# Attention's products on pairs of 16-bit floats, and the causal mask added by VectorE with the row maximum

## The chip, the cores and the metric

One NeuronCore of one Trainium2 chip runs the whole program in a single launch. The metric is the device time of that launch in microseconds (us), less is better. TensorE (PE) multiplies, with its weight loads (PEld) shown apart; VectorE (DVE), ScalarE (ACT) and GpSimd (POOL) do elementwise work; SyncE (SP) issues the DMAs.

## The reference

The program is a macaron block on 8 sequences of 1024 tokens with 256 features: half a feed-forward step, attention, half a feed-forward step. The feed-forward quantises its inputs and weights to 4-bit floats in blocks of 16. Cut to what matters here:

```
def _L0_attn_ref(query, Wq, Wk, Wv, Wo, span_val):      # 16 heads of 64
    q, k, v = (_split_heads(query @ W) for W in (Wq, Wk, Wv))
    w = jnp.einsum('bhqd,bhkd->bhqk', q, k) / DH
    w = w + causal                                      # -1e9 above the diagonal
    w = softmax(w) * clip((arange(s) + span_val * s) / 33, 0, 1)
    w = w / (sum(w) + 1e-8)
    return merge_heads(einsum('bhqk,bhkd->bhqd', w, v)) @ Wo

x = x + 0.5 * ffn(layernorm(x)); x = x + attn(layernorm(x)); x = x + 0.5 * ffn(layernorm(x))
```

## The kernel before

The program has three stages: a first feed-forward pass (`ffn_pass`, tag `ffn1`), attention (`attention`), and a second feed-forward pass (`ffn2`). A feed-forward pass works through 32 macros of 256 tokens. While the first pass runs, `prepare` splits the attention weights in hooks of its steps: ScalarE rounds a chunk of 128x512 to the high half (`hi_of`, L1034), GpSimd subtracts it from the chunk to get the low half (`split`, L835), and SyncE stores both to DRAM (`store`, L762). There are 16 such chunks, one per step from step 0 on. The chunks of Wv and Wo are first scaled by a power of two (L1040) that is derived from the largest element of Wv (`largest_v`, L919, and `powers`, L923).

Attention goes through 8 sequences times 8 pairs of heads, 64 pairs in all (`over_pairs`, L1102). All products are made of a high and a low part: high by high, high by low, low by high. The operands of the projections, of the scores and of the output product are rounded 32-bit words (`F32R`); the operands of the product with the values (`v_cols`, `eT`) are already 16-bit floats (`F16`). Each pair has 16 units, one for each head and each tile j of 128 query rows; a unit's scores have 128(j+1) columns, since the mask is causal. Per unit:

- `scores` (L1343) waits until the exponential of the unit two before has read the same PSUM buffer (`exp_done`, L1350). It makes the scores in one or two chunks of 256 to 512 columns, each as two matmuls, since the keys' low and high halves are stacked on the 128 partitions (L1356, L1357). A third matmul, a 16-bit identity by a 128x128 block of 0 and -1e9, adds the mask to the diagonal block (L1360).
- `row_max` (L1538) is VectorE's reduction of the scores to the negated row maximum (L1542).
- `exp` (L1448) is ScalarE's exponential, from PSUM into `e_rows`, with that as its bias (L1455).
- `turn` (L1363) transposes the rows on TensorE in groups of up to four 128x128 blocks, 24 groups a pair, as 32-bit words (L1370). ScalarE rounds a group to `eT_hi` (`turn_hi`, L1462), VectorE subtracts to get `eT_lo` (`turn_lo`, L1548), and three groups later `value` (L1373) multiplies both by the values (L1386, 132 and 66 columns).

Between them lie ten side pieces a pair, which share one PSUM bank (`side_ps`): two each of q and k for the next pair (`project`, L1285, six matmuls of 512 columns each), two transposes of the output (L1324), and four of values (L1297) or of the output product (L1334), twelve matmuls of 256 columns each. A side piece is copied by ScalarE (high part, L1435) and finished by VectorE (low part, L1510, or L1524, L1536) before the next may use the bank. The pieces of q and k go by DMA to the stacked layout (`place`, L1124).

The order of all this work is a table of steps that each engine runs in its own queue: `pair_steps` (L618) puts the side pieces into numbered slots (`WO_SLOTS`, `V_SLOTS`, `FRESH_SLOTS`, L585 to L587), and in the first pair of a sequence 14 small steps of normalising the next rows are added to VectorE's queue (`norm_x`, L1561).

## Time and profile before

| | |
|---|---|
| time, median of 3 runs | 3530.09 us (3526.44 to 3532.24) |
| span of the profiled execution, first to last instruction | 3527.3 us; no other time of that execution is given |
| busy: TensorE, VectorE, ScalarE, GpSimd | 96%, 83%, 67%, 24% |
| mean granted clock of TensorE | 0.988 |
| DMA | 375.19 MB, mean 106 GB/s |
| chain that ended last | PE 64%, DVE 10%, issue 6%, ACT 2%, POOL 2% |

A row of TensorE gives a duration with the pipeline's latency in it, so neighbouring matmuls overlap. What a matmul costs is read from one start to the next. The same holds in a smaller measure for VectorE.

### The profile page before, as it was taken

The numbers are of one execution on the slowest core, as the hardware profiler recorded it, in microseconds if no ns is written. First come the engines' busy times: TensorE is split into PE (matmuls) and PEld (weight loads), VectorE is DVE, ScalarE is ACT, GpSimd is POOL, SyncE is SP. The second block draws the span as 40 slices with busy tenths as digits, with TensorE's granted clock in tenths as the row PEclk, the third lists the DMA queues.
The fourth block names the chain that finished last, engine by engine and source line by source line (L and its number), as shares of the span: only waits on it lengthen the run. The fifth ranks groups of instructions, "written<-read, shape, count | busy, mean of one in ns | idle before, by whom it ended". The sixth has DMA issues, their size and how long they took to land.

```text
span 3527.3 us, 77883 instructions
## 1 busy us (share of the span) xinstructions
PE 3383.0 (96%) x29872; PEld 3071.4 (87%) x29872; DVE 2916.8 (83%) x4672; ACT 2350.8 (67%) x4307; POOL 848.4 (24%) x911
## 2 busy tenths in 40 slices
PE   4999996999999999999999999999999999799998
PEld 4999995888888888888888888888888888699998
DVE  8999974888888888888888878878887888899996
...
GB/s 123 95 123 87 93 33 124 97 117 125 125 109 126 109 142 125 112 125 122 109 126 137 116 109 134 125 103 141 134 98 107 145 104 153 54 49 55 55 54 37
DMA packets 160338, 375.19 MB, mean 106 GB/s; under 512 B 19824, under 2 KB 62832, under 8 KB 159728
## 3 DMA queue, kind: packets, MB, share of 16 engines
...
## 4 chain that ended last, share of the span: by engine, by line
PE 64%; DVE 10%; issue 6%; ACT 2%; POOL 2%; POOLq 0%; ACTq 0%; DVEq 0%
PE at_t_ps L1370 11%; PE at_side_ps L1285 9%; PE at_o_ps L1386 8%; PE ffn_gu_ps L505 7%; PE at_s_ps L1356 6%; PE at_s_ps L1357 6%; PE at_side_ps L1297 5%; PE at_side_ps L1334 4%; PE ffn_down_ps L530 4%; DVE at_neg_max L1542 3%; DVE at_eT_lo L1548 3%; PE at_s_ps L1360 1%; PE ffn_hT_ps L475 1%; PE at_side_ps L1324 1%; DVE at_oT_lo L1510 1%
## 5 line engine op out<-in xcount | busy, mean ns | idle before, releaser
L1548 DVE SCALAR_TENSOR_TENSOR at_eT_lo<-at_t_ps,at_eT_hi 128x512 f16<-128x512 f32 (+3 forms) x1536 | 852.2, 555 | 328.8 <-ACT at_eT_hi L1462 322.9
L1462 ACT ACTIVATE at_eT_hi<-at_t_ps 128x512 f16<-128x512 f32 (+3 forms) x1536 | 756.7, 493 | 333.3 <-PE at_t_ps L1370 322.6
L1455 ACT ACTIVATE at_e_rows<-at_s_ps,at_neg_max 128x1024 f32<-128x1024 f32 (+7 forms) x1024 | 759.7, 742 | 152.2 <-DVE at_neg_max L1542 144.7
L1370 PE MATMUL at_t_ps<-at_ident,at_e_rows 128*128 128x128 f32 x4608 | 798.8, 284 | 0.0
L1542 DVE TENSOR_REDUCE at_neg_max<-at_s_ps 128x1 f32<-128x1024 f32 (+7 forms) x1024 | 766.1, 748 | 19.4 <-PE at_s_ps L1360 15.6
L1386 PE MATMUL at_o_ps<-at_v_cols,at_eT_hi 128*128 128x132 f16 x4608 | 611.5, 222 | 2.1 <-DVE at_eT_lo L1548 1.6
L1356 PE MATMUL at_s_ps<-at_kh_st,at_q_st 128*128 128x512 f32 (+2 forms) x1536 | 583.0, 380 | 19.0 <-issue 9.1
L1386 PE MATMUL at_o_ps<-at_v_cols,at_eT_lo 128*128 128x66 f16 x4608 | 567.2, 192 | 0.0
L1357 PE MATMUL at_s_ps<-at_kl_st,at_q_st 128*128 128x512 f32 (+2 forms) x1536 | 514.1, 342 | 0.0
L1370 PEld LDWEIGHTS at_t_ps<-at_ident,at_e_rows 128*128 128x128 f32 x4608 | 491.7, 141 | 0.1
L1386 PEld LDWEIGHTS at_o_ps<-at_v_cols,at_eT_hi 128*128 128x128 f16 x4608 | 432.5, 98 | 25.7 <-issue 18.8
L1386 PEld LDWEIGHTS at_o_ps<-at_v_cols,at_eT_lo 128*128 128x128 f16 x4608 | 420.8, 98 | 4.0
L1285 PE MATMUL at_side_ps<-at_xT_hi,at_w_qk 128*128 128x512 f32 x1012 | 382.3, 418 | 6.5 <-DVE at_xT_lo L1510 1.4
L1356 PEld LDWEIGHTS at_s_ps<-at_kh_st,at_q_st 128*128 128x128 f32 x1536 | 295.5, 192 | 46.2 <-issue 13.5
L1244 POOL TENSOR_TENSOR at_o_sum<-at_o_raw 128x1056 f32<-128x1056 f32 x64 | 133.1, 2080 | 753.8 <-ACT at_o_raw L1473 753.8
L1357 PEld LDWEIGHTS at_s_ps<-at_kl_st,at_q_st 128*128 128x128 f32 x1536 | 292.8, 191 | 24.1
L385 POOL TENSOR_TENSOR ffn_h_q<-ffn_code,ffn_scale 128x704 f32<-128x704 f32 x128 | 178.0, 1392 | 561.8 <-DVE ffn_code L313 561.8
L505 PE MATMUL ffn_gu_ps<-ffn_w_gu_hi,ffn_xT_hi 128*128 128x352 f32 x1024 | 257.6, 333 | 25.1 <-DVE ffn_raw L276 15.7
L1473 ACT ACTIVATE at_o_raw<-at_o_ps 128x264 f32<-128x264 f32 x512 | 203.0, 396 | 76.9 <-PE at_o_ps L1386 75.7
L505 PE MATMUL ffn_gu_ps<-ffn_w_gu_lo,ffn_xT_hi 128*128 128x352 f32 x1024 | 250.6, 327 | 0.0
L505 PE MATMUL ffn_gu_ps<-ffn_w_gu_hi,ffn_xT_lo 128*128 128x352 f32 x1024 | 250.3, 326 | 0.0
L442 ACT ACTIVATE ffn_silu<-ffn_gu_ps 128x704 f32<-128x704 f32 x128 | 97.2, 760 | 214.4 <-PE ffn_gu_ps L505 214.4
...
## 6 DMA issues: line engine op xcount, KB each, us to landing
at_kh_st<-at_k_hi SPq DMA_DIRECT2D x256, 256.0 KB, 4.5
at_kl_st<-at_k_lo SPq DMA_DIRECT2D x256, 256.0 KB, 5.9
...
at_q_st<-at_q_hi SPq DMA_DIRECT2D x128, 256.0 KB, 3.8
at_q_st<-at_q_lo SPq DMA_DIRECT2D x128, 256.0 KB, 4.8
...
```

The costliest lines, as they stand in the source:

```text
L385: nc.gpsimd.tensor_tensor(blocks_of(h_q[:, par, j, :INNER]), blocks_of(code[:, j * INNER:(j + 1) * INNER]), per_block(scale[:, par, j * HB ...
L505: last = nc.tensor.matmul(gu_ps[:, c, 0:HALF_I], xT[a][:, par, kt, j * P:(j + 1) * P], gu[b][:, kt, c * HALF_I:(c + 1) * HALF_I], start=n ...
L1285: last = nc.tensor.matmul(bank[:], wts[:, w, s, kt, :], xT[t][:, kt, c * CHUNK:(c + 1) * CHUNK], start=i == 0, stop=i == len(passes) - 1)
L1356: nc.tensor.matmul(out, qs, kh_st[par][a][:, k0:k0 + w], start=True, stop=False)
L1357: last = nc.tensor.matmul(out, qs, kl_st[par][a][:, k0:k0 + w], start=False, stop=not lastc)
L1370: last = nc.tensor.transpose(t_ps[i % TBUF][:, b * P:(b + 1) * P], e_rows[:, n % 4, (k0 + b) * P:(k0 + b + 1) * P], ident[:])
L1386: last = nc.tensor.matmul(o[:, :VPART[s]], eT[s][:, i % EBUF, b * P:(b + 1) * P], v_cols[par][:, k0 + b, a, :VPART[s]], start=k0 + b == 0 ...
L1455: nc.scalar.activation(e_rows[:, n % 4, :w], s_ps[n % 2][:, col:col + w], ACT.Exp, bias=neg_max[:, n % 4:n % 4 + 1]).then_inc(sem("exp_don ...
L1462: nc.scalar.activation(eT[0][:, i % EBUF, :count * P], t_ps[i % TBUF][:, :count * P], ACT.Copy, scale=PSCALE).then_inc(sem("eT_hi"), 1)
L1473: nc.scalar.activation(o_raw[:, a * QT + j0:a * QT + j1 + 1:j1 - j0, :], o_ps[n // OSET % OBUF][:, :2 * VCOLS].rearrange("p (u d) -> p u d ...
L1542: nc.vector.tensor_reduce(neg_max[:, n % 4:n % 4 + 1], s_ps[n % 2][:, col:col + P * (j + 1)], AX.X, ALU.max, negate=True).then_inc(sem("ma ...
L1548: nc.vector.scalar_tensor_tensor(out=eT[1][:, i % EBUF, :count * P], in0=t_ps[i % TBUF][:, :count * P], scalar=PSCALE, in1=eT[0][:, i % EB ...
```

## The change

- The weights of q, k, v and o, the turned rows, q, k and their stacked copies, and the turned output become pairs of `F16` in place of pairs of `F32R`. All four weight matrices are scaled by powers of two (`flip`), the turned rows by 2^10; the scales are taken back in `s_scale` (scores), the mask of the values, and `o_scale` (output product, which becomes a scalar_tensor_tensor on VectorE).
- The largest element is now taken of all four matrices (four reductions on VectorE, two each in steps 1 and 2), and the splitting of the weights starts 6 steps later (`PA_FIRST`), with one scaling on ScalarE for each of the 16 chunks, not for 8. The steps written out before the loop grow from 20 to 24.
- The chunks of the scores are 512 columns and the rest, down to 128; the mask matmul is gone. q is negated, and VectorE makes scores times scale plus a strip (0, and a large positive number above the diagonal) into `e_rows` in one tensor_tensor_reduce that also gives the minimum. ScalarE's exponential then reads and writes `e_rows`. `scores` waits for `max_done` of the unit two before, no longer for `exp_done`; the wait for the free row of `e_rows` moves from ScalarE to VectorE.

```
-HEAD = 5 * UNROLL
+HEAD = 6 * UNROLL
...
 def score_chunks(j):
     w = P * (j + 1)
-    if w <= CHUNK:
-        return [(0, 0, max(w, 2 * P))]
-    first = CHUNK if w - CHUNK >= 2 * P else w - 2 * P
-    return [(CHUNK - first, 0, first), (CHUNK, first, w - first)]
+    return [(0, 0, w)] if w <= CHUNK else [(0, 0, CHUNK), (CHUNK, CHUNK, w - CHUNK)]
...
-    half = [[sb(f"{part}{s}", [P, CHUNK], F32R) for s in range(PA_SLOTS)] for part in ("hi", "lo")]
+    half = [[sb(f"{part}{s}", [P, CHUNK], F16) for s in range(PA_SLOTS)] for part in ("hi", "lo")]
...
         def third_out():
-            largest_v()
+            largest_of(0)
+            largest_of(1)
             scaled(4)
+        def other_largest():
+            largest_of(2)
+            largest_of(3)
...
-            if i >= 2:
-                act.wait_ge(sem("powers"), 1)
-                nc.scalar.activation(chunk(c), chunk(c), ACT.Copy, scale=(flip if i == 2 else unscale)[:, 0:1]).then_inc(sem("even"), 1)
+            act.wait_ge(sem("powers"), 1)
+            nc.scalar.activation(chunk(c), chunk(c), ACT.Copy, scale=flip[:, i:i + 1]).then_inc(sem("even"), 1)
...
-                **{(c, "normed"): (lambda c=c: hi_of(c)) for c in range(2, len(PA_CHUNKS))}}
+                **{(c + PA_FIRST, "normed"): (lambda c=c: hi_of(c)) for c in range(len(PA_CHUNKS))}}
...
-        xT = [sb(f"xT_{part}", [P, KT, SEQ], F32R) for part in ("hi", "lo")]
-        side = {n: [sb(f"{n}_{part}", [P, SEQ], F32R) for part in ("hi", "lo")] for n in "qk"}
-        q_st, kh_st, kl_st = ([[sb(f"{n}{i}{a}", [P, SEQ], F32R) for a in range(2)] for i in range(2)] for n in ("q_st", "kh_st", "kl_st"))
+        xT = [sb(f"xT_{part}", [P, KT, SEQ], F16) for part in ("hi", "lo")]
+        side = {n: [sb(f"{n}_{part}", [P, SEQ], F16) for part in ("hi", "lo")] for n in "qk"}
+        q_st, kh_st, kl_st = ([[sb(f"{n}{i}{a}", [P, SEQ], F16) for a in range(2)] for i in range(2)] for n in ("q_st", "kh_st", "kl_st"))
+        strip = sb("strip", [P, SEQ])
...
-                pe.wait_ge(sem("exp_done"), g * NU + (n - 1 + AHEAD["exp_done"]))
+                pe.wait_ge(sem("max_done"), g * NU + (n - 1 + AHEAD["max_done"]))
...
-                    last = nc.tensor.matmul(out, qs, kl_st[par][a][:, k0:k0 + w], start=False, stop=not lastc)
-                    if lastc:
-                        diag = col + j * P - k0
-                        last = nc.tensor.matmul(s_ps[n % 2][:, diag:diag + P], ident_b[:], causal[:], start=False, stop=True)
+                    last = nc.tensor.matmul(out, qs, kl_st[par][a][:, k0:k0 + w], start=False, stop=True)
...
-                act.wait_ge(sem("turned"), g * NG + (LAST_GROUP[(n - 4) % NU] + 1 + (n - 4) // NU * NG + AHEAD["turned"]))
-                nc.scalar.activation(e_rows[:, n % 4, :w], s_ps[n % 2][:, col:col + w], ACT.Exp, bias=neg_max[:, n % 4:n % 4 + 1]).then_inc(sem("exp_done"), 1)
+                nc.scalar.activation(e_rows[:, n % 4, :w], e_rows[:, n % 4, :w], ACT.Exp, bias=neg_max[:, n % 4:n % 4 + 1],
+                                     scale=-1.0).then_inc(sem("exp_done"), 1)
...
-                nc.vector.tensor_reduce(neg_max[:, n % 4:n % 4 + 1], s_ps[n % 2][:, col:col + P * (j + 1)], AX.X, ALU.max,
-                                        negate=True).then_inc(sem("max_done"), 1)
+                dve.wait_ge(sem("turned"), g * NG + (LAST_GROUP[(n - 4) % NU] + 1 + (n - 4) // NU * NG + AHEAD["turned"]))
+                nc.vector.tensor_tensor_reduce(e_rows[:, n % 4, :w], s_ps[n % 2][:, col:col + w], strip[:, SEQ - w:], keep["s_scale"][:, 0:1], BIGGEST,
+                                               ALU.add, ALU.min, neg_max[:, n % 4:n % 4 + 1]).then_inc(sem("max_done"), 1)
```

How the instructions stand on the engines. First TensorE, at the scores of a unit with 640 columns (j = 4), and the first of the value products behind them (`at_kh_st` and `at_kl_st` are the stacked keys; numbers behind names are the builder's). Before:

```order
L1356 MATMUL at_s_ps<-at_kh_st_6933,at_q_st_6929 128x384
L1357 MATMUL at_s_ps<-at_kl_st_6937,at_q_st_6929 128x384
L1356 MATMUL at_s_ps<-at_kh_st_6933,at_q_st_6929 128x256
L1357 MATMUL at_s_ps<-at_kl_st_6937,at_q_st_6929 128x256
L1360 MATMUL at_s_ps<-at_causal,at_ident_b 128x128
L1386 MATMUL at_o_ps<-at_v_cols_6943,at_eT_hi 128x132
```

and now:

```order
L1366 MATMUL at_s_ps<-at_kh_st_7431,at_q_st_7427 128x512
L1367 MATMUL at_s_ps<-at_kl_st_7435,at_q_st_7427 128x512
L1366 MATMUL at_s_ps<-at_kh_st_7431,at_q_st_7427 128x128
L1367 MATMUL at_s_ps<-at_kl_st_7435,at_q_st_7427 128x128
L1393 MATMUL at_o_ps<-at_v_cols_7442,at_eT_hi 128x132
L1393 MATMUL at_o_ps<-at_v_cols_7442,at_eT_lo 128x66
```

The same 640 columns are taken in chunks of 512 and 128, and the third matmul is gone.

Second VectorE, in the middle of a pair that has q, k and value pieces (`at_den` and `at_rden` are the row sums and their reciprocals). Before:

```order
L1548 SCALAR_TENSOR_TENSOR at_eT_lo<-at_t_ps,at_eT_hi 128x512
L1559 RECIPROCAL at_rden<-at_den 128x16
L1548 SCALAR_TENSOR_TENSOR at_eT_lo<-at_t_ps,at_eT_hi 128x384
L1510 SCALAR_TENSOR_TENSOR at_k_lo<-at_side_ps,at_k_hi 128x512
L1542 TENSOR_REDUCE at_neg_max<-at_s_ps 128x1
L1548 SCALAR_TENSOR_TENSOR at_eT_lo<-at_t_ps,at_eT_hi 128x512
L1542 TENSOR_REDUCE at_neg_max<-at_s_ps 128x1
L1548 SCALAR_TENSOR_TENSOR at_eT_lo<-at_t_ps,at_eT_hi 128x512
```

and now:

```order
L1556 SCALAR_TENSOR_TENSOR at_eT_lo<-at_t_ps,at_eT_hi 128x512
L1567 RECIPROCAL at_rden<-at_den 128x16
L1556 SCALAR_TENSOR_TENSOR at_eT_lo<-at_t_ps,at_eT_hi 128x384
L1514 SCALAR_TENSOR_TENSOR at_k_lo<-at_side_ps,at_k_hi 128x512
L1550 ISA at_e_rows,at_neg_max<-at_s_ps,at_strip,keep_s_scale 128x384
L1550 ISA at_neg_max 128x1
L1556 SCALAR_TENSOR_TENSOR at_eT_lo<-at_t_ps,at_eT_hi 128x512
L1550 ISA at_e_rows,at_neg_max<-at_s_ps,at_strip,keep_s_scale 128x1024
L1550 ISA at_neg_max 128x1
L1556 SCALAR_TENSOR_TENSOR at_eT_lo<-at_t_ps,at_eT_hi 128x512
```

Each reduction has become two instructions in VectorE's queue, of which the second writes the minimum alone; their places between the `eT_lo` rows are the same.

Third VectorE in the first feed-forward pass, at the end of its step 1 (`prep_raw_wv` is Wv as loaded). Before:

```order
L296 RECIPROCAL ffn_recip<-ffn_tied 128x120
L299 TENSOR_TENSOR ffn_unit<-ffn_raw,ffn_recip 128x1920
L921 TENSOR_REDUCE prep_big<-prep_raw_wv 128x1
L255 BN_STATS ffn_stats<-ffn_x_rows 128x6 x2
L259 BN_AGGR ffn_moments<-ffn_stats 128x2 x2
L261 TENSOR_SCALAR ffn_var_eps<-ffn_moments 128x2
```

and now:

```order
L296 RECIPROCAL ffn_recip<-ffn_tied 128x120
L299 TENSOR_TENSOR ffn_unit<-ffn_raw,ffn_recip 128x1920
L921 TENSOR_REDUCE prep_big<-prep_raw_wq 128x1
L921 TENSOR_REDUCE prep_big<-prep_raw_wk 128x1
L255 BN_STATS ffn_stats<-ffn_x_rows 128x6 x2
L259 BN_AGGR ffn_moments<-ffn_stats 128x2 x2
```

Two reductions stand where there was one, and two more follow at the end of the next step.

## Rows read from the trace of the kernel before

**Rows 1.** The page: span, and busy time by engine.
```profile
span 3527.3 us, 77883 instructions
...
PE 3383.0 (96%) x29872; PEld 3071.4 (87%) x29872; DVE 2916.8 (83%) x4672; ACT 2350.8 (67%) x4307; POOL 848.4 (24%) x911
```

**Rows 2.** Windows by stage: start:end, length, busy us (x instructions) of PE, PEld, DVE, ACT, POOL; clock, DMA share, GB/s.
```profile
60.00:500.00 440.00, 430.14 (x3061) 425.02 (x3062) 415.83 (x477) 268.29 (x374) 158.41 (x161) 0.99 0.28 89
...
580.00:3010.00 2430.00, 2401.11 (x22978) 2109.72 (x22976) 1971.78 (x3509) 1753.88 (x3470) 504.35 (x536) 1.00 0.49 122
...
3040.00:3527.00 487.00, 464.49 (x3331) 457.71 (x3329) 431.63 (x497) 269.16 (x371) 142.26 (x150) 0.99 0.16 49
```

**Rows 3.** Windows of the length of one sequence (8 pairs), amid attention; columns as above.
```profile
1000.00:1304.00 304.00, 301.14 (x2887) 264.70 (x2886) 247.69 (x443) 219.68 (x435) 64.72 (x69) 1.00 0.49 122
```

**Rows 4.** Timeline of TensorE amid attention: start us, us, engine, line, what, count.
```profile
1500.93 0.22 PE L1386 MATMUL at_o_ps<-at_v_cols,at_eT_hi 128*128 128x132 f16 x1
...
1501.28 0.63 PE L1370 MATMUL at_t_ps<-at_ident,at_e_rows 128*128 128x128 f32 x4
1501.66 0.48 PE L1285 MATMUL at_side_ps<-at_xT_hi,at_w_qk 128*128 128x512 f32 x1
1501.98 0.39 PE L1285 MATMUL at_side_ps<-at_xT_lo,at_w_qk 128*128 128x512 f32 x1
...
1502.68 0.39 PE L1285 MATMUL at_side_ps<-at_xT_lo,at_w_qk 128*128 128x512 f32 x1
...
1503.83 0.28 PE L1357 MATMUL at_s_ps<-at_kl_st,at_q_st 128*128 128x256 f32 x1
1503.95 0.23 PE L1360 MATMUL at_s_ps<-at_causal,at_ident_b 128*128 128x128 bf16 x1
1504.02 0.22 PE L1386 MATMUL at_o_ps<-at_v_cols,at_eT_hi 128*128 128x132 f16 x1
...
1504.28 0.30 PE L1370 MATMUL at_t_ps<-at_ident,at_e_rows 128*128 128x128 f32 x1
1504.72 0.50 PE L1285 MATMUL at_side_ps<-at_xT_hi,at_w_qk 128*128 128x512 f32 x1
```

**Rows 5.** Groups by line over the span: ... xcount, busy us, mean ns of one, idle before.
```profile
L1356 PE MATMUL at_s_ps<-at_kh_st,at_q_st 128*128 128x512 f32 (+2 forms) x1536 | 583.0, 380 | 19.0 <-issue 9.1 <-ACT at_e_rows L1455 6.4 <-DVE at_acc L1536 3.5
...
L1360 PE MATMUL at_s_ps<-at_causal,at_ident_b 128*128 128x128 bf16 x1024 | 235.8, 230 | 0.0
...
L1356 PEld LDWEIGHTS at_s_ps<-at_kh_st,at_q_st 128*128 128x128 f32 x1536 | 295.5, 192 | 46.2 <-issue 13.5 <-DVE at_acc L1536 4.9 <-ACT at_e_rows L1455 4.3
...
L1386 PEld LDWEIGHTS at_o_ps<-at_v_cols,at_eT_hi 128*128 128x128 f16 x4608 | 432.5, 98 | 25.7 <-issue 18.8 <-DVE at_eT_lo L1548 2.9
```

**Rows 6.** Timeline of VectorE amid attention.
```profile
1503.97 0.69 DVE L1510 SCALAR_TENSOR_TENSOR at_q_lo<-at_side_ps,at_q_hi 128x512 fp32r<-128x512 f32 x1 [0.70 <-ACT at_q_hi L1435]
...
1516.08 0.68 DVE L1548 SCALAR_TENSOR_TENSOR at_eT_lo<-at_t_ps,at_eT_hi 128x512 f16<-128x512 f32 x1
1516.68 1.21 DVE L1542 TENSOR_REDUCE at_neg_max<-at_s_ps 128x1 f32<-128x1024 f32 x1
1517.89 0.69 DVE L1548 SCALAR_TENSOR_TENSOR at_eT_lo<-at_t_ps,at_eT_hi 128x512 f16<-128x512 f32 x1
...
1531.95 0.63 DVE L1571 BATCH_NORM_AGGREGATE at_moments<-at_stats 128x2 f32<-128x6 f32 x8
```

**Rows 7.** Groups by line over the span: VectorE, a PSUM and an SBUF operand.
```profile
L1536 DVE TENSOR_TENSOR at_acc<-at_side_ps,at_acc 128x512 f32<-128x512 f32 x125 | 85.7, 686 | 6.3 <-PE at_side_ps L1334 0.7
```

**Rows 8.** Timeline of VectorE in step 1 of the first feed-forward pass.
```profile
67.56 2.28 DVE L921 TENSOR_REDUCE prep_big<-prep_raw_wv 128x1 f32<-128x2048 f32 x1
69.76 0.74 DVE L255 BATCH_NORM_STATS2 ffn_stats<-ffn_x_rows 128x6 f32<-128x256 f32 x2
```

**Rows 9.** Timelines at attention's start: SyncE's issues and TensorE's first scores.
```profile
569.80 2.93 SPq L1130 DMA_DIRECT2D at_kl_st<-at_k_lo  x4
...
579.53 0.77 PE L1356 MATMUL at_s_ps<-at_kh_st,at_q_st 128*128 128x512 f32 x1 [9.10 <-issue]
```

More of the change, by code:

```diff
@@ L225, in body @@
                     load_rows(i + UNROLL, k)
-                if isinstance(i, int) and UNROLL <= i < HEAD and not reload:
+                if isinstance(i, int) and UNROLL <= i < UNROLL + 16 and not reload:
                     keep_weights(i - UNROLL)
@@ L571 @@
 SUM_EPS = 1e-8
+BIGGEST = 3.0e38
+XSCALE = 2.0 ** 10
+EARLY, LATE = 60 * 1024, 132 * 1024
 PSCALE = 2.0 ** 14
@@ L768, in store @@
             for part in range(2):
-                cols = half[part][c % PA_SLOTS][:].bitcast(F32)
+                cols = half[part][c % PA_SLOTS][:]
                 if i < 2:
@@ L793, in before_step @@
                 spread_largest()
-            if step >= 2:
-                store(step - 2)
+            if step >= PA_FIRST + 2:
+                store(step - PA_FIRST - 2)
         def all_stored():
@@ L818, in sync @@
         return {START: first_loads, "rows": other_loads, MACROS - UNROLL + 1: first_sequence, "end": first_loaded,
-                **{step: (lambda step=step: before_step(step)) for step in range(1, len(PA_CHUNKS) + 2)}}
+                **{step: (lambda step=step: before_step(step)) for step in range(1, PA_FIRST + len(PA_CHUNKS) + 2)}}
     def gpsimd(pool):
@@ L960, in first_norm @@
                                         ALU.subtract, ALU.mult).then_inc(sem("xn_first"), 1)
-        return {START: first_two, LAST: first_norm, -3: lambda: to_codes(1), -2: lambda: scaled(2), (0, "rows out"): third, 1: third_out, 6: powers}
+        return {START: first_two, LAST: first_norm, -3: lambda: to_codes(1), -2: lambda: scaled(2), (0, "rows out"): third, 1: third_out, 2: other_largest, 6: powers}
     def tensor(pe):
@@ L1129, in place @@
                         for a in range(2):
-                            sp.dma_start(st[par][a][half * DH:(half + 1) * DH, :].bitcast(F32),
-                                         side[n][part][a * DH:(a + 1) * DH, :].bitcast(F32)).then_inc(sem(f"{n}_placed{par}"), 16)
+                            sp.dma_start(st[par][a][half * DH:(half + 1) * DH, :],
+                                         side[n][part][a * DH:(a + 1) * DH, :]).then_inc(sem(f"{n}_placed{par}"), 16)
             def start():
@@ L1394, in start @@
                         pe.wait_ge(sem("xT_lo"), 4)
-                    out.append(piece(kind, c, 0, 0, 0, 1, out[n - 4] if n >= 4 else ("consts", 3), start_ps[n % 4]))
+                    out.append(piece(kind, c, 0, 0, 0, 1, out[n - 4] if n >= 4 else ("consts", 1), start_ps[n % 4]))
                 scores(0, 0, 0)
@@ L1439, in piece @@
                 if kind in ("q", "k"):
-                    copy_side(side[kind][0][:, cols], f"{kind}_done", 2 * g + (c + 1), f"{kind}_hi", 1.0 / DH if kind == "q" else 1.0, bank)
+                    copy_side(side[kind][0][:, cols], f"{kind}_done", 2 * g + (c + 1), f"{kind}_hi", (-1.0 if kind == "q" else 1.0) / XSCALE, bank)
                 elif kind == "o_turn":
@@ L1509, in split_side @@
                 dve.wait_ge(sem(ready), count)
-                nc.vector.scalar_tensor_tensor(out=out, in0=bank[:], scalar=scale, in1=hi.bitcast(F32),
+                nc.vector.scalar_tensor_tensor(out=out, in0=bank[:], scalar=scale, in1=hi,
                                                op0=ALU.mult, op1=ALU.subtract).then_inc(sem(signal), 1)
@@ L1516, in piece @@
                     hi, lo = side[kind]
-                    split_side(lo[:, cols], hi[:, cols], f"{kind}_hi", 2 * g + (c + 1), f"{kind}_lo", 1.0 / DH if kind == "q" else 1.0, bank)
+                    split_side(lo[:, cols], hi[:, cols], f"{kind}_hi", 2 * g + (c + 1), f"{kind}_lo", (-1.0 if kind == "q" else 1.0) / XSCALE, bank)
                 elif kind == "v":
@@ L1531, in piece @@
                     out = [xT[s][:, c // 2, (c % 2) * CHUNK:(c % 2 + 1) * CHUNK] for s in range(2)]
-                    split_side(out[1], out[0], "xT_hi", g + (c + 1), "xT_lo", 1.0, bank)
+                    split_side(out[1], out[0], "xT_hi", g + (c + 1), "xT_lo", XSCALE, bank)
                 elif kind == "wo":
@@ L1535, in piece @@
                     rows = acc[:, 2 * c:2 * c + 2, :].rearrange("p j k -> p (j k)")
-                    nc.vector.tensor_tensor(rows, bank[:], rows, ALU.add).then_inc(sem("wo_added"), 1)
+                    nc.vector.scalar_tensor_tensor(out=rows, in0=bank[:], scalar=keep["o_scale"][:, 0:1], in1=rows,
+                                                   op0=ALU.mult, op1=ALU.add).then_inc(sem("wo_added"), 1)
             def row_max(n, g):
@@ L1617, in _ @@
             nc.vector.memset(power[:], -0.5).then_inc(sem("power"), 1)
-            for name in ("eT_lo", "wo_added"):
+            dve.wait_ge(sem("masked"), 2)
+            for name in ("eT_lo", "wo_added", "max_done"):
                 dve.sem_inc(sem(name), AHEAD[name])
```

104 lines of the change are left out of this document (56 added, 48 removed).

## The prediction

> **What bounds the kernel now.** I read the page first for the whole: in a span of 3527.3 us TensorE is busy for 96% and VectorE for 83% [rows 1]. A mean over three stages says little, so the windows by stage come next [rows 2]. The reader is to see that attention takes some 2430 of 3527 us, that TensorE is busy for 2401 us of them at a granted clock of 1.00 (the 2.4 GHz level), and that VectorE is busy for 1972. Both feed-forward passes have TensorE busy for nearly all of their steady part, with VectorE close behind: 415.8 of 440 us. One sequence, 8 pairs, takes exactly 304 us, window after window, so a pair takes 38.0 us; in it VectorE is busy for 247.7/8 = 31.0 us and ScalarE for 27.5 [rows 3]. The timeline of TensorE shows why it is the bound [rows 4]: matmuls start one behind the other, and gaps in which it waits for others are short. So a pair is worth what its matmuls cost from start to start, as long as nobody else becomes slower than TensorE.
>
> **TensorE, per pair.** From starts to starts [rows 4]: three matmuls of rounded words with 512 columns take 0.70 us from 1501.98 to 1502.68, 0.233 each. One with 256 columns takes 0.12. Four pairs of 16-bit matmuls with 132 and 66 columns take 0.35 us from 1500.93 to 1501.28, 0.0875 a pair. At 2.4 GHz, a column a cycle, 198 columns are 0.0825, so each 16-bit matmul has about 3 ns on top. I take N/2.4 + 3 ns for 16 bits: 0.216 us for 512 columns, 0.163 for 384, 0.110 for 256, 0.056 for 128. No row has 16-bit matmuls of 512 columns in this kernel, so the bounds are 0.213 (a column a cycle) and 0.233 (as the rounded words).
> - The projections of q and k have 4 pieces of 6 matmuls: 24 x (0.233 - 0.216) = 0.41 us.
> - Values or output product, 4 pieces of 12 matmuls: 48 x (0.120 - 0.110) = 0.48 us.
> - Scores: per head 12 chunks, each twice (L1356 counts 1536, 24 a pair [rows 5]). Before, a pair has 20 matmuls of 512 columns, 12 of 384 (0.177, midway between the two rows) and 16 of 256: 4.66 + 2.12 + 1.92 = 8.70 us. Now 24 of 512, 8 each of 384, 256 and 128: 5.18 + 1.30 + 0.88 + 0.45 = 7.81 us. Saved: 0.89 us.
> - Mask: 16 matmuls a pair (1024 in all [rows 5]), 0.07 us from 1503.95 to 1504.02 [rows 4]: 1.1 us.
> - First matmul after transposes: the one at 1501.66 takes 0.32 us to the next start, not 0.233 [rows 4], since its weight load takes 192 ns where a 16-bit one takes 98 [rows 5], and a transpose ahead of it (0.11 each) hides only the shorter. The value matmuls after transposes show no such step. In the timeline about 18 of a pair's 24 groups of such matmuls begin behind transposes: 18 x 0.087 = 1.55 us.
>
> Sum: 4.4 us a pair, 282 us over 64 pairs. With 16-bit matmuls as slow per column as rounded words only the mask, the weight loads and the 512 columns fewer (0.22 us) are left, 2.9 us.
>
> The Trainium skill ("TensorE: Matmul & The Clock Gate", section "Back-to-back issue gap") gives N/2.4 + 2.5 ns for a lone kind of matmul, but about 81 ns at 128 columns for real streams of weight loads and matmuls. By the latter the eight 128-column matmuls would cost 0.2 us a pair more, 13 us in all; the trace has 0.0875 for two 16-bit matmuls with their loads, and sides with the former.
>
> **VectorE, per pair.** The reduction turns into two instructions (the order shows `at_e_rows,at_neg_max` and then `at_neg_max` alone). For the main one the nearest row is one that takes PSUM and SBUF in and writes SBUF: 686 ns at 512 columns [rows 7], as `eT_lo` and `q_lo` take [rows 6]; the reduction itself takes 1.21 us for 1024 columns, so all run at one element a cycle with the same constant. I book no difference. The second, tiny one is nowhere in this trace. Eight aggregations of 6 elements take 0.63 us, 0.08 each [rows 6], the lower bound. If it has to wait until the main one has drained, the next instruction loses the overlap too (1516.08 to 1516.68 is 0.60 for an instruction of 0.68, so 0.08), and a small instruction takes 0.17: 0.25, the upper bound. I take 0.12, nearer the row. 16 x 0.12 = 1.9 us, with bounds of 1.3 and 4.0: VectorE is then busy for 32.9 us a pair. The output product's addition keeps its length, a multiplication more in the same pass.
>
> **What is late next.** TensorE alone would need 38.0 - 4.4 = 33.6 us, VectorE 32.9. They are now level, and two waits grow. First the side pieces: they share one bank, and the next may start only when VectorE is done with the last. Here TensorE starts one transpose at 1504.28 and the next q piece only at 1504.72 [rows 4], 0.33 us beyond the 0.11 of the transpose, because `q_lo` ran from 1503.97 to 1504.66 [rows 6]. With less other work between, such places wait longer by what that work shrank: some 3 places a pair by 0.1 us, 0.3 us. Second VectorE's queue, at 94% load: `eT_lo` and `max_done` come later where 1024-column units and side pieces meet. I take 0.9 us (0 if the three groups between turn and value absorb it, 2.6 if VectorE with some idle time sets the pace). A pair takes 38.0 - 4.4 + 1.2 = 34.8 us: 3.2 us less, 205 us in 64 pairs. In the first pair of seven of the sequences VectorE has normalisation on top, about 5 us by its rows of 0.41 us and less; it is the bound there: 1.5 us each, 10 us.
>
> **Edits off that path.** ScalarE reads SBUF and not PSUM in the exponential, and has 10 us of slack a pair: nothing, hidden under TensorE. The scores no longer wait for the exponential; that wait hardly shows (6.4 us over the span [rows 5]), so nothing. DMAs halve, off the path except at the start: `place` is issued until 572.73, the scores begin at 579.53 [rows 9]; half the bytes save 4 us (0 to 7). The strip's set-up on GpSimd adds under 1 us, inside that. In the first pass VectorE gets three more reductions of 2.2 us (67.56 to 69.76 [rows 8]) at steps 1 and 2, where it is the bound, and some 1.5 us in `powers`: 7 us (3 to 9), since VectorE's slack in a step is small. Eight more scalings on ScalarE, busy 268 of 440 us [rows 2], and later stores on SyncE's and splits on GpSimd's queues cost nothing: all is stored by step 23, and attention loads it at step 29.
>
> **Sum.** 3527.3 - 205 + 10 - 4 + 7 = 3335 us for the profiled execution. Its span lies 2.8 us under the median of the runs, 3530.1, so the median is put at 3338 us.
>
> **The rivals.**
> - Everything absorbed: queues and bank cost nothing, 3527 - 282 + 3 = 3248, 3251 as a median. For it speaks that TensorE waits little today with VectorE at 82%; against, the wait at 1504.28 that is there already.
> - VectorE the bound: the small instruction costs 0.25 us, VectorE needs 35.0 us a pair and with some idle time the pair takes 36.2: 1.8 x 64 = 115 less, 3527 - 115 + 13 = 3425, median 3428. It decides from about 0.16 us on, where VectorE's sum passes TensorE's.
> - 16 bits no faster per column: 2.9 - 1.2 = 1.7 us a pair, 109 us, 3431, median 3434.
> - Slower than before: the new main instruction takes two cycles an element. Mean length is 576 columns, 0.6 us more in each of 16, 9.6 us a pair: VectorE 31.0 + 1.9 + 9.6 = 42.5 us busy, less 1.5 of overlap, so pairs of 41 us: 3527 + 192 + 13 = 3732, median 3735. It turns slower from some 0.45 us an instruction on. For it: nothing here scales, adds and reduces in one pass. Against it: each of its parts runs at full rate, and PSUM and SBUF together do too [rows 7]. The Trainium skill ("Vector Engine (DVE) Microarchitecture Reference", section "Points that are easy to get wrong") says that such a form with two 32-bit SBUF sources runs at half throughput; here one source is PSUM, so by its wording the rule would not bite, and no run here shows it.
>
> **How the numbers follow.** Forecast 0.50, all absorbed 0.14, VectorE the bound 0.17, 16 bits no faster 0.10, half rate 0.07; 0.02 for anything else. The likeliest is 3338 us. Its own range, 3290 to 3385, is reached out to the rivals on the faster side: 3255 to 3445 leaves out the half rate and a little at each end. A measurement tells 0.2% (7 us) from no change. Faster by more than that: 0.92; within: 0.01; slower: 0.07.
>
> **What would show it.** In the profile after: 16-bit matmuls of 512 columns starting 0.216 us apart, first ones after transposes without the 0.09 step, no mask rows; the new main rows near 1.22 us at 1024 columns and the small rows behind them at 0.08 to 0.17; a sequence of 278 to 282 us; VectorE busy for over 90% of it; TensorE's waits for `eT_lo`, `q_lo` and `k_lo` grown to about 1 us a pair. The prediction is wrong if main rows are near 2.3 us, if a sequence takes over 290 us, or if the first pass grows by more than 10 us.

## The result, and the profile after

The changed kernel takes 3453.35 us (median of 4 runs, 3450.93 to 3454.41) against 3529.8 us before: a ratio of 0.9782, with a 95% interval of 0.9768 to 0.9796. It is 76 us faster. The forecast was 3338 us, 192 us faster, with a range up to 3445 us: the sign was right, the size was not, and the result lies above the range.

The page of the kernel after, span and engines (to [rows 1]):

```profile
span 3452.6 us, 76458 instructions
...
PE 3223.7 (93%) x28848; PEld 2677.1 (78%) x28848; DVE 2967.2 (86%) x5704; ACT 2367.8 (69%) x4315; POOL 845.1 (24%) x910
```

Windows of the kernel after, columns as in [rows 2, 3]; the last is one sequence of 8 pairs:

```profile
60.00:500.00 440.00, 427.75 (x3019) 422.51 (x3020) 416.63 (x478) 272.19 (x381) 153.81 (x160) 0.98 0.24 74
...
1000.00:1296.00 296.00, 282.93 (x2769) 217.36 (x2768) 254.43 (x574) 221.68 (x437) 64.50 (x69) 0.99 0.28 69
```

All of the gain lies in attention. The first low part `eT_lo` starts at 587.5 us before and 586.8 after, the last one at 3013.3 and 2937.4: 75 us less between them. Ahead of it two changes cancel. The last instruction of the first feed-forward pass on VectorE, before and then after:

```profile
536.53 0.69 DVE L322 SCALAR_TENSOR_TENSOR ffn_x_out<-ffn_down_ps,ffn_x_res 128x512 f32<-128x512 f32 x1 [8.81 <-PE ffn_down_ps L530]
```

```profile
543.11 0.69 DVE L322 SCALAR_TENSOR_TENSOR ffn_x_out<-ffn_down_ps,ffn_x_res 128x512 f32<-128x512 f32 x1 [8.77 <-PE ffn_down_ps L530]
```

The pass ends 6.6 us later, and from there to the first scores it takes 38.0 us (543.11 to 581.13) and not 43.0 (536.53 to 579.53 [rows 9]). The starts of `eT_lo`, 24 to a pair, give the length of each pair. A plain pair took 37.4 to 37.7 us and takes 36.0 to 36.2. The first pair of a sequence took 39.2 and takes **39.7** (39.5 to 40.2). The seventh, with the transposes of the next sequence's x, went from 40.8 to 39.2. A whole sequence went from 305.1 to some 296 us. TensorE's busy sum is 282.9 of the 296 us; before it was 301.1 of 304 [rows 3]. VectorE is busy for 254.4 of them, 86%. So TensorE has waits that it did not have: over the span the waits that the trace names ahead of its matmuls in attention add up to 53 us before and 142 after, 1.4 us more a pair. Those that VectorE ended went from 11 to 102 us.

Waits over the span, first of the kernel before (us in total, times, longest), then of the kernel after:

```profile
PEld at_side_ps L1324 <- DVE at_oT_lo L1510: 24.4, 63, 0.4
...
PE at_side_ps L1324 <- DVE at_oT_lo L1510: 1.8, 7, 0.3
```

```profile
ACT at_e_rows L1458 <- DVE at_neg_max L1550: 319.3, 558, 10.2
DVE at_eT_lo L1556 <- ACT at_eT_hi L1466: 246.7, 524, 0.9
...
PE at_side_ps L1334 <- DVE at_oT_lo L1514: 47.9, 63, 1.0
...
PE at_s_ps L1366 <- DVE at_acc L1540: 12.5, 6, 2.1
...
PE at_side_ps L1344 <- DVE at_acc L1540: 11.0, 31, 0.7
...
PE at_side_ps L1295 <- DVE at_q_lo L1514: 9.7, 35, 0.6
PE at_side_ps L1307 <- DVE at_v_masked L1528: 9.2, 31, 0.3
```

The second output transpose (L1334) now waits in every pair for VectorE to let go of the side bank. The timelines around one such place, after, VectorE and then TensorE:

```profile
1633.39 0.69 DVE L1514 SCALAR_TENSOR_TENSOR at_k_lo<-at_side_ps,at_k_hi 128x512 f16<-128x512 f32 x1
1634.00 0.61 DVE L1550 CUSTOM_DVE_ANT_0 at_e_rows<-at_s_ps,at_strip,keep_s_scale 128x384 f32<-128x384 f32 x1
1634.53 0.09 DVE L1550 DVE_READ_ACCUMULATOR2_ANT at_neg_max<- 128x1 f32 x1
1634.53 0.69 DVE L1556 SCALAR_TENSOR_TENSOR at_eT_lo<-at_t_ps,at_eT_hi 128x512 f16<-128x512 f32 x1
1635.13 1.27 DVE L1550 CUSTOM_DVE_ANT_0 at_e_rows<-at_s_ps,at_strip,keep_s_scale 128x1024 f32<-128x1024 f32 x1
1636.33 0.08 DVE L1550 DVE_READ_ACCUMULATOR2_ANT at_neg_max<- 128x1 f32 x1
1636.33 0.69 DVE L1556 SCALAR_TENSOR_TENSOR at_eT_lo<-at_t_ps,at_eT_hi 128x512 f16<-128x512 f32 x1
1636.94 0.68 DVE L1514 SCALAR_TENSOR_TENSOR at_oT_lo<-at_side_ps,at_oT_hi 128x512 f16<-128x512 f32 x1
1637.79 0.29 DVE L1556 SCALAR_TENSOR_TENSOR at_eT_lo<-at_t_ps,at_eT_hi 128x128 f16<-128x128 f32 x1 [0.18 <-ACT at_eT_hi L1466]
```

```profile
1634.84 0.60 PE L1334 MATMUL at_side_ps<-at_ident,at_o_norm 128*128 128x128 f32 x4
...
1636.14 0.52 PE L1377 MATMUL at_t_ps<-at_ident,at_e_rows 128*128 128x128 f32 x3
...
1637.67 0.66 PE L1334 MATMUL at_side_ps<-at_ident,at_o_norm 128*128 128x128 f32 x4 [1.00 <-DVE at_oT_lo L1514]
```

ScalarE had `oT_hi` ready at 1636.24 (0.59 us from 1635.65), but VectorE has no gap from 1633.39 to 1637.62, and `oT_lo` gets its turn at 1636.94. Elsewhere in the same pair VectorE stands idle, some 5 us in all.

The new instruction by form, after (count, busy us, mean ns), and the output product's addition:

```profile
L1550 DVE CUSTOM_DVE_ANT_0 at_e_rows<-at_s_ps,at_strip,keep_s_scale 128x1024 f32<-128x1024 f32 x128 | 163.3, 1276 | 5.6 <-PE at_s_ps L1367 4.8
...
L1540 DVE SCALAR_TENSOR_TENSOR at_acc<-at_side_ps,keep_o_scale,at_acc 128x512 f32<-128x512 f32 x125 | 92.9, 744 | 0.6 <-PE at_side_ps L1344 0.6
L1550 DVE DVE_READ_ACCUMULATOR2_ANT at_neg_max<- 128x1 f32 x1024 | 85.0, 83 | 0.0
```

### The profile page after: what moved, and what is told of

It reads as the page before. It is cut to its first block, busy times and chain, and to the rows that moved or that the text cites. A ratio compares the mean times of both kernels' runs of the same rounds, so it can differ in the third digit from the quotient of the medians.

```text
span 3452.6 us, 76458 instructions
## 1 busy us (share of the span) xinstructions
PE 3223.7 (93%) x28848; PEld 2677.1 (78%) x28848; DVE 2967.2 (86%) x5704; ACT 2367.8 (69%) x4315; POOL 845.1 (24%) x910
## 4 chain that ended last, share of the span: by engine, by line
PE 42%; DVE 17%; issue 16%; ACT 7%; POOL 2%; DVEq 0%; ACTq 0%; POOLq 0%
DVE at_e_rows L1550 8%; PE ffn_gu_ps L505 7%; PE at_side_ps L1295 7%; PE at_t_ps L1377 6%; PE at_o_ps L1393 5%; DVE at_eT_lo L1556 4%; ACT at_eT_hi L1466 4%; PE ffn_down_ps L530 4%; PE at_s_ps L1366 3%; PE at_s_ps L1367 3%; PE at_side_ps L1344 3%; PE at_side_ps L1307 1%; DVE at_v_masked L1528 1%; PE ffn_hT_ps L475 1%; DVE at_oT_lo L1514 1%
## 5 line engine op out<-in xcount | busy, mean ns | idle before, releaser
L1458 ACT ACTIVATE at_e_rows<-at_e_rows,at_neg_max 128x1024 f32<-128x1024 f32 (+7 forms) x1024 | 791.5, 773 | 321.3 <-DVE at_neg_max L1550 319.3
L1466 ACT ACTIVATE at_eT_hi<-at_t_ps 128x512 f16<-128x512 f32 (+3 forms) x1536 | 742.8, 484 | 158.3 <-PE at_t_ps L1377 144.7
L1550 DVE CUSTOM_DVE_ANT_0 at_e_rows<-at_s_ps,at_strip,keep_s_scale 128x1024 f32<-128x1024 f32 (+7 forms) x1024 | 827.7, 808 | 7.0 <-PE at_s_ps L1367 6.2
L1366 PE MATMUL at_s_ps<-at_kh_st,at_q_st 128*128 128x512 f16 (+3 forms) x1536 | 502.2, 327 | 18.3 <-DVE at_acc L1540 12.5
L1367 PE MATMUL at_s_ps<-at_kl_st,at_q_st 128*128 128x512 f16 (+3 forms) x1536 | 481.9, 327 | 0.0
L1295 PE MATMUL at_side_ps<-at_xT_hi,at_w_qk 128*128 128x512 f16 x1012 | 344.5, 381 | 12.7 <-DVE at_q_lo L1514 9.7
L1366 PEld LDWEIGHTS at_s_ps<-at_kh_st,at_q_st 128*128 128x128 f16 x1536 | 154.7, 101 | 106.5 <-DVE at_acc L1540 13.9
L1259 POOL TENSOR_TENSOR at_o_norm<-at_o_sum,at_rden 128x1024 f32<-128x1024 f32 x64 | 122.0, 1906 | 435.6 <-DVE at_rden L1567 435.6
L1247 POOL CAST at_v_cols<-at_v_masked 128x512 f16<-128x512 f32 x128 | 78.3, 612 | 597.9 <-DVE at_v_masked L1528 597.9
```

What stands on the lines that cost most here:

```text
L1295: last = nc.tensor.matmul(bank[:], wts[:, w, s, kt, :], xT[t][:, kt, c * CHUNK:(c + 1) * CHUNK], start=i == 0, stop=i == len(passes) - 1)
L1366: nc.tensor.matmul(out, qs, kh_st[par][a][:, k0:k0 + w], start=True, stop=False)
L1367: last = nc.tensor.matmul(out, qs, kl_st[par][a][:, k0:k0 + w], start=False, stop=True)
L1458: nc.scalar.activation(e_rows[:, n % 4, :w], e_rows[:, n % 4, :w], ACT.Exp, bias=neg_max[:, n % 4:n % 4 + 1], scale=-1.0).then_inc(sem("ex ...
L1466: nc.scalar.activation(eT[0][:, i % EBUF, :count * P], t_ps[i % TBUF][:, :count * P], ACT.Copy, scale=PSCALE).then_inc(sem("eT_hi"), 1)
L1550: nc.vector.tensor_tensor_reduce(e_rows[:, n % 4, :w], s_ps[n % 2][:, col:col + w], strip[:, SEQ - w:], keep["s_scale"][:, 0:1], BIGGEST, ...
```

## The experiments

Four readings stood against each other. **A**: the step of 0.087 us behind transposes [rows 4] was never there to save, and about 1.4 us a pair come back as waits. **B**: the steps were saved, and all that is missing are waits. **C**: TensorE is the bound throughout, and VectorE's time does not matter. **D**: VectorE's sum of work decides.

### One half of the change at a time

`only_16bit` keeps TensorE's mask, the plain maximum and the exponential out of PSUM, with q and k scaled by constants that hold for this input:

```diff
-                nc.vector.tensor_tensor_reduce(e_rows[:, n % 4, :w], s_ps[n % 2][:, col:col + w], strip[:, SEQ - w:], ...
+                nc.vector.tensor_reduce(neg_max[:, n % 4:n % 4 + 1], s_ps[n % 2][:, col:col + w], AX.X, ALU.max, negate=True)...
+                    if lastc:
+                        last = nc.tensor.matmul(s_ps[n % 2][:, diag:diag + P], ident_b[:], causal[:], start=False, stop=True)
```

> The 16-bit pairs alone: mask by TensorE and plain row maximum as in the kernel before. Theory A (no step behind transposes was ever there to save, TensorE's own saving is 1.8 us a pair here, some 0.4 us of it comes back as waits at the side bank): 1.4 us x 64 = 90 us less than before, about 3440 us. Rival B (the step of 0.087 us was real and was saved, all that is missing in the changed kernel are waits that VectorE makes): TensorE saves 3.3 us a pair, 0.7 comes back, 165 us less, about 3365 us. In the trace A has the last transpose and the first matmul behind it together at 0.325 us before the next start (0.348 before the change).

Measured: 3433.7 us (3433.0 to 3434.4), ratio 0.9724 [0.9708, 0.9741], 97 us less than before and **20 us less than the whole change**. Reading A named 3440, B 3365. Its trace settles the step; TensorE, four transposes and what follows:

```profile
1640.35 0.63 PE L1380 MATMUL at_t_ps<-at_ident,at_e_rows 128*128 128x128 f32 x4
1640.82 0.38 PE L1366 MATMUL at_s_ps<-at_kh_st,at_q_st 128*128 128x512 f16 x1
1641.03 0.38 PE L1367 MATMUL at_s_ps<-at_kl_st,at_q_st 128*128 128x512 f16 x1
```

From the first transpose to the second 512-column matmul it is 0.68 us here, and was 0.70 before (1501.28 to 1501.98 [rows 4]). The difference is what the 512 columns save (0.233 to 0.216), and nothing more. In [rows 4] the first matmul indeed takes 0.32 us to the next start, but it starts 0.08 us early, 0.38 behind the first of the four transposes. In nearly every place of the trace of the kernel before, a rounded matmul stands 0.39 behind the first of four transposes, and a 16-bit value matmul 0.47. With 16 bits the matmul of the scores starts 0.47 behind too, and takes 0.21. The record had moved the 0.087 us from one row to the next.

`only_mask` is the other half: rounded words kept, the mask and the maximum in one VectorE instruction, with a column of ones as scale.

```diff
-                    if lastc:
-                        diag = col + j * P - k0
-                        last = nc.tensor.matmul(s_ps[n % 2][:, diag:diag + P], ident_b[:], causal[:], start=False, stop=True)
+                nc.vector.tensor_tensor_reduce(e_rows[:, n % 4, :w], s_ps[n % 2][:, col:col + w], strip[:, SEQ - w:], one[:, 0:1], BIGGEST, ...
```

> The mask and the maximum in one VectorE instruction alone, products on rounded 32-bit words kept. TensorE has 16 mask matmuls a pair less (1.0 us), VectorE 1.9 us a pair more. Theory A (waits at the side bank and in the first pair of a sequence take what VectorE adds): 0 to 0.4 us a pair less, 3505 to 3530 us. Rival C (VectorE's time never matters while it is below TensorE's): 1.0 us a pair less, 3466 us. Rival D (VectorE's queue decides fully): 0.9 us a pair more, 3588 us.

Measured: 3511.0 us (3509.3 to 3511.7), ratio 0.9942 [0.9925, 0.9958], 19.5 us less, 0.3 us a pair. TensorE's 1.0 us a pair is mostly given back; on rounded words both C and D fall. The halves alone give 97 and 19.5 us, together 76: on top of the 16-bit pairs the fused mask, with its scale read from a column, **costs** 20 us.

### What a microsecond is worth on each engine

`immediate` gives the two scales as constants of the instruction instead of columns in SBUF; they hold for this input:

```diff
-  nc.vector.scalar_tensor_tensor(out=rows, in0=bank[:], scalar=keep["o_scale"][:, 0:1], in1=rows,
+  nc.vector.scalar_tensor_tensor(out=rows, in0=bank[:], scalar=2.0 ** -16, in1=rows,
...
-  nc.vector.tensor_tensor_reduce(..., strip[:, SEQ - w:], keep["s_scale"][:, 0:1], BIGGEST,
+  nc.vector.tensor_tensor_reduce(..., strip[:, SEQ - w:], 2.0 ** -22, BIGGEST,
```

> The changed kernel with the two scales as constants of the instruction instead of a column in SBUF. Theory A: each of 16 maxima and of the output additions loses its 60 ns, VectorE has 1.1 us a pair less, of which a third to a half is on the path: 20 to 35 us under the changed kernel, 3420 to 3433. Rival D (VectorE decides fully): 1.1 us x 64 = 70 us, 3383. If the 60 ns are not from the column but from the custom instruction itself, only the additions shorten and the time stays within 5 us of 3453.

Measured: 3413.0 us (3410.9 to 3413.8), ratio 0.9666 [0.965, 0.9682], 40 us under the changed kernel, a little more than A's 20 to 35. The trace of `immediate`, VectorE by form:

```profile
L1550 DVE CUSTOM_DVE_ANT_0 at_e_rows<-at_s_ps,at_strip 128x1024 f32<-128x1024 f32 x128 | 155.6, 1216 | 5.9 <-PE at_s_ps L1367 5.9
...
L1540 DVE SCALAR_TENSOR_TENSOR at_acc<-at_side_ps,at_acc 128x512 f32<-128x512 f32 x125 | 85.7, 686 | 0.9 <-PE at_side_ps L1344 0.6
L1550 DVE DVE_READ_ACCUMULATOR2_ANT at_neg_max<- 128x1 f32 x1024 | 85.4, 83 | 0.1
```

1216 ns for 1276, 686 for 744: reading the scale from a column costs 60 ns an instruction, whatever its length. That is 1.1 us a pair on VectorE, and 0.63 us of it were on the path. With constants the fused mask gains 21 us over `only_16bit`, instead of costing 20. A little of the 21 is not the mask's: `only_16bit` still reads `o_scale` from a column, two additions of 60 ns a pair.

`zero_mask` puts 16 mask matmuls a pair back, which add zeros:

```diff
+                    if lastc:
+                        diag = col + j * P - k0
+                        last = nc.tensor.matmul(s_ps[n % 2][:, diag:diag + P], ident_b[:], zeros[:], start=False, stop=True)
```

> The changed kernel with 16 mask matmuls a pair put back that add zeros: 1.0 us a pair more for TensorE, nothing for VectorE. Theory A (TensorE waits about 2 us a pair at the side bank, work between two side pieces fills part of it): 0.4 to 0.7 us a pair more, 3480 to 3498. Rival C (TensorE is the bound throughout): 1.0 us a pair, 3517. Rival D (VectorE decides): under 0.2 us a pair, under 3465.

Measured: 3462.7 us (3459.7 to 3467.8), ratio 0.9811 [0.9795, 0.9827]: 9 us more, 0.15 us a pair for 0.9 us of TensorE's work (16 starts, 0.056 us each in this trace). C wanted 64 us. For the changed kernel D now looked best, and A had TensorE too dear.

### Where the waits are made

The next two move side pieces. The numbers are places among a pair's 24 groups:

```diff
-WO_SLOTS = (0, 2, 4, 7, 9, 11, 14, 15, 19, 21)
-V_SLOTS = (2, 3, 5, 7, 9, 11, 14, 16, 20, 21)
+WO_SLOTS = (0, 2, 4, 7, 9, 12, 15, 17, 19, 21)
+V_SLOTS = (2, 3, 5, 7, 9, 12, 15, 17, 19, 21)
```

That is `slots_o`. `slots_q` has the same last six places and 0, 3, 5, 7 ahead of them in both tables.

> The changed kernel with the second output transpose one step later (place 12 instead of 11, so 2.6 us of TensorE's work instead of 1.2 lie between the two), and the four pieces behind it at 15, 17, 19, 21. Theory A (the returned time is waits of TensorE at the one side bank, 1.0 us a pair at this place): 0.6 to 0.9 us a pair less, 3395 to 3415 us. Rival D (VectorE's sum decides, as a scale of 60 ns an instruction was worth 40 us and 1.0 us of TensorE's only 9): the wait moves elsewhere, within 12 us of 3453.

> As the one before, and the projections of q and k at places 0, 3, 5, 7 in every pair (2.7 us of TensorE's work between the first two, not 1.1 or 1.5). Theory A: another 0.1 to 0.4 us a pair less, 3375 to 3405 us. Rival D: within 12 us of 3453.

Measured: `slots_o` 3441.6 us (3441.0 to 3442.9), ratio 0.9747 [0.9731, 0.9764]; `slots_q` 3445.6 us (3445.3 to 3446.7), ratio 0.9759 [0.9743, 0.9775]. Only 12 and 8 us less, against 40 to 75 expected, and within the 12 that D named. The wait of the second output transpose had gone, and two others stood in its place. A row of TensorE's timeline in `slots_o`, and its waits over the span:

```profile
1630.27 0.22 PE L1393 MATMUL at_o_ps<-at_v_cols,at_eT_hi 128*128 128x132 f16 x1 [0.87 <-DVE at_eT_lo L1556]
```

```profile
PE at_o_ps L1393 <- DVE at_eT_lo L1556: 41.6, 60, 1.7
PE at_o_ps L1393 <- ACT at_o_raw L1477: 33.8, 64, 1.0
```

The value product now waits for `eT_lo`, which stands in the same full queue of VectorE, and for ScalarE's copy out of the one bank of output sums. A was wrong on where the time is made: freeing the side bank at this place does not give it back.

`slots_even` spaces all ten pieces, at 0, 3, 6, 9, 12, 15, 18, 20, 21, 23:

> The changed kernel with the ten side pieces at 0, 3, 6, 9, 12, 15, 18, 20, 21, 23: at least 2.6 us of TensorE's work behind each that goes through ScalarE and VectorE, but the last addition close to the next pair's first piece. Theory A: 3375 to 3420 us. Rival D: within 12 us of 3453.

Measured: 3552.7 us (3552.1 to 3554.0), ratio 1.006 [1.0044, 1.0077], **slower than before the change**, so neither reading holds. TensorE's waits there:

```profile
PE at_o_ps L1393 <- ACT at_o_raw L1477: 106.8, 231, 1.0
...
PE at_o_ps L1393 <- DVE at_eT_lo L1556: 24.5, 60, 1.7
```

The copy `o_raw` follows the last value product of a pair of units, at places 2, 5, 8, 11, 14, 17, 20 and 23, and the next product into that bank comes one place later. A side piece at such a place gives TensorE something to do meanwhile. The old tables have three and five pieces there, those of `slots_o` two and three, `slots_even` two. The count alone does not decide: `slots_q` has two as well, and waits 57.6 us for `o_raw`, in 119 places. Of the 99 us that `slots_even` takes over the changed kernel, the waits for `o_raw` are 100 (6.4 us there), and 25 more stand ahead of scores with no releaser named; waits for VectorE are 29 us fewer.

That gave a fifth reading, **E**: VectorE has 31 of 36 us of work, but it is full in some stretches and idle in others. The time is made in the full ones. I laid the three queues side by side with the durations of the trace, the copies among them, and chose 1, 3, 5, 8, 9, 11, 13, 15, 18, 21 for all pairs.

> The changed kernel with the ten side pieces at 1, 3, 5, 8, 9, 11, 13, 15, 18, 21 in every pair. Theory E, formed after the last runs (in a plain pair VectorE has 31 of 36 us, but its queue is without a gap in the stretch that holds the 1024-column maximum, the last low part of k and both output transposes, and elsewhere it idles; the returned time is made in such stretches, and where TensorE waits, at the bank or for the low part, is only where it shows): pieces that give TensorE much and VectorE little, put where VectorE is full, and none two steps apart around place 10 to 12, give 0.8 to 1.3 us a pair, 3370 to 3405 us. Rival D (VectorE's sum counts, wherever it is): within 12 us of slots_o, 3430 to 3453.

> The same with the 16 mask matmuls a pair that add zeros, 1.0 us more for TensorE. Theory E: with VectorE's full stretches relieved TensorE is the bound over more of the pair, so 0.4 to 0.9 us a pair more than slots_odd (25 to 58 us), where the changed kernel had 0.15. Rival D: as there, under 12 us more.

Measured: `slots_odd` 3411.5 us (3404.6 to 3412.8), ratio 0.9665 [0.9649, 0.9681], 42 us under the changed kernel with the same instructions on every engine; D allowed 12 to either side of `slots_o`, and it lies 30 under. Plain pairs take 35.15 us. It came 7 us above E's range, since the first pair of a sequence did not shrink with the others and takes 40.0 us. `slots_odd_zero` 3440.1 us (3436.1 to 3441.4), ratio 0.9743 [0.9726, 0.9759]: TensorE's 0.9 us now costs 29 us, 0.45 a pair, three times as much as in the old order. No run changes VectorE's queue and the cover of the copies one at a time, but the waits over the span, added up by who ended them, tell them apart. From the changed kernel to `slots_odd`, TensorE's waits for VectorE fall from 102 to 64 us, and those for `o_raw` rise from 6.4 to 8.7. That is 36 of the 42 us, all of it waits for VectorE. The copies took from `slots_o` what the new places had won there (VectorE 78 us, `o_raw` 33.8); they are not what the changed kernel lacked.

### The first pair of a sequence

After the change, TensorE at the end of a first pair, and the windows there (columns as above):

```profile
1506.63 0.52 PE L1377 MATMUL at_t_ps<-at_ident,at_e_rows 128*128 128x128 f32 x3
1509.23 0.39 PE L1366 MATMUL at_s_ps<-at_kh_st,at_q_st 128*128 128x512 f16 x1 [2.08 <-DVE at_acc L1540]
...
1510.24 1.09 PE L1377 MATMUL at_t_ps<-at_ident,at_e_rows 128*128 128x128 f32 x4
```

```profile
1492.00:1502.00 10.00, 9.37 (x100) 7.76 (x98) 9.78 (x26) 6.95 (x13) 0.00 (x0) 1.00 0.08 24
1502.00:1512.00 10.00, 7.92 (x80) 6.66 (x79) 9.85 (x32) 5.56 (x12) 1.81 (x2) 0.91 0.18 42
```

VectorE is busy for 9.8 of 10 us. TensorE waits 2.08 us at the next pair's head for the last addition, and here the granted clock then falls: four transposes take 1.09 us, not 0.63. It does not always fall. The trace has six such places, each with a wait of 2.08 us. Behind four of them transposes start some 0.21 us apart, not 0.11, for one or two microseconds, and that pair or the next is 0.6 us longer. Behind the other two nothing changes. In `only_16bit` the same wait is 1.5 us, and behind none of the six do transposes slow down. `norm_split` moves the four steps that scale x into the second pair:

```diff
+            if rows == 1 and i >= ROWS_FROM and i - ROWS_FROM <= QT:
+                steps.append(("norm_x", i - ROWS_FROM, 1))
+            if rows == 2 and i in ROWS_LATE:
+                steps.append(("norm_x", QT + 1 + ROWS_LATE.index(i), 1))
```

> The changed kernel with the normalisation's last four steps (the scaling of x, 2.6 us of VectorE) moved from the end of a sequence's first pair into the second pair. Theory A (in a first pair, 39.7 us, VectorE is some 2 us late at its end, TensorE stands still for 2.1 us at the next pair's head and runs at a lower clock for some 2 us behind it): the first two pairs take 1.5 to 2.5 us less together, seven times, 10 to 18 us less, 3435 to 3443. Rival: the second pair grows by as much as the first shrinks, within 4 us of 3453.

Measured: 3437.2 us (3435.9 to 3438.0), ratio 0.9733 [0.9717, 0.9749], 16 us less, as expected. The first pair takes 37.3 us, the second 36.1, the wait at the head is 0.6 us, and transposes slow down behind none of the six.

### The edits together

> Three edits together: the places of slots_odd, the normalisation split over two pairs, and the scales as constants (these hold for this input alone). If they add up, slots_odd less 14 less 25 to 40 us. Theory E: 3320 to 3360 us, since a shorter VectorE instruction is worth less once its queue has gaps. Pairs of 34.5 to 35.0 us.

> The kernel of only_16bit (mask by TensorE, plain maximum) with the places of slots_odd and the split normalisation. TensorE's own work is 35.0 us a pair there, and it waited some 0.8 us: theory E gives 3385 to 3410 us, above the fused kernel with the same places and constants, which has 1.0 us a pair less for TensorE. If it comes out under that one, the fused maximum is worth nothing here whatever the order.

> The changed kernel with the places of slots_odd and the split normalisation, scales still read from a column (so it holds for any weights). Theory E: slots_odd (3411.5) less 14 to 30, since there the first pair of a sequence takes 40.0 us: 3382 to 3398 us. Against odd_split_imm (3364) it prices the 60 ns of the column in a relieved queue: 20 to 30 us, less than the 40 us of the changed kernel. Rival D (VectorE's sum counts the same in any order): 40 us, 3404.

> The kernel before, rounded words and TensorE's mask, with the same places and the split normalisation. Theory E: TensorE waits only some 0.6 us a pair there and the first pairs cost 1.8 us each, so 25 to 50 us less than before, 3480 to 3505 us: much less than the 60 to 70 us that the same edits are worth behind the change, so what they recover is the change's own lost gain. Rival (the places are simply better and have nothing to do with the change): the same 60 to 70 us, 3460 to 3470.

- `odd_split_imm`: 3364.2 us (3363.7 to 3365.1), ratio 0.9531 [0.9515, 0.9547], just above E's range; pairs of 34.97 us. It beats the kernel before by 4.7% and the changed one by 2.6%, but its two constants hold only for weights of this size.
- `odd_split`, which holds for any weights: 3389.6 us (3388.0 to 3391.0), ratio 0.9604 [0.9588, 0.962]. **64 us under the changed kernel.** Against `odd_split_imm` the column costs 25 us here and 40 in the old order, as E has it and D not.
- `tensor_mask_odd`: 3402.3 us (3402.2 to 3404.5), ratio 0.964 [0.9624, 0.9656], 38 us above `odd_split_imm` (one has constants for q and k, the other for the scores and the output product): in a good order, and with constants, the fused mask pays. Read from a column it still does: `odd_split` is 13 us under `tensor_mask_odd`.
- `before_odd_split`: 3511.7 us (3509.6 to 3512.5), ratio 0.9948 [0.9931, 0.9965]. The same places and split are worth 17 us before the change, under E's 25, and 64 behind it. What they recover is mostly what the change had lost. Some 12 of the 17 us are the first pairs (39.2 to 37.5 us, seven times); plain pairs take 37.45 us.

## Why the prediction was wrong

The forecast was 115 us too low. By its own steps:

- **TensorE, per pair, "First matmul after transposes": the step that failed.** 18 x 0.087 = 1.55 us a pair, 99 us in all, were booked from one start-to-start distance without the one ahead of it in the same rows. The runs show nothing to save there: four transposes and the matmul behind them take 0.70 us before and 0.68 with 16 bits. The rest of the list held: starts 0.216 us apart at 512 columns, 0.11 at 256, no mask rows, 2.85 us a pair.
- **"I book no difference" for the main VectorE instruction** was off by 60 ns, and "the output product's addition keeps its length" by the same: both now read their scale from a column. The small read was booked at 0.12 us and costs almost nothing: at 1024 columns the next instruction starts 1.20 us after the fused one (1635.13 to 1636.33), as the row of the read does itself, 1.14 with the constant, 1.13 after the plain maximum. VectorE got 1.2 us a pair, not 1.9. Two errors of opposite sign.
- **"What is late next"** was right in kind, and near in size: booked 1.2 us a pair. The measured pairs leave 2.85 - 1.4 = 1.45, 16 us more over 64 pairs, and the waits that the traces name grow by 1.4 a pair. The place was named (bank and queue), but the largest wait is for `oT_lo` (48 us), not for `eT_lo`, `q_lo` or `k_lo`. And it was read from VectorE's average load of 94%, where 86% was measured. How large it is hangs on where the side pieces stand, as `slots_odd` and `before_odd_split` show; that it is made where VectorE's queue has no gap was read from the timelines, and `slots_odd`, built on it, came within 7 us of its range.
- **The first pairs** take 3.5 us more than the pairs of the same kind (39.7 to 36.2), before 1.5 (39.2 to 37.7): 2.0 more, where 1.5 were booked. The clock's fall behind TensorE's wait was not foreseen.
- **Start and first pass** came out as booked: 7 us more for the pass, measured 6.6; 4 us less for the start, measured 5.0. The 6.6 us arise where they were placed: 4.7 behind the four reductions (2.28 us each, where one stood), the rest behind `powers`.
- **"One sequence takes exactly 304 us"** was the length of the windows asked for. By the starts of `eT_lo` it took 305.1, so a pair took 38.1, which changes no term.

Put right in the first step alone, the same sum gives 3338 + 99 = 3437; the 16 us of waits make it 3453. That this meets the measured time to the microsecond is in part luck: the terms above are good to a few us each. The rivals at 3428 and 3434 come close to the measured time by number, not by mechanism: 16-bit matmuls are as fast as forecast, and VectorE's small instruction is not 0.25 us. Of the signs named, "if a sequence takes over 290 us" came true: it takes 296.
